# Sixteen transposes of the identity on TensorE ahead of the first real matmul of a graph network kernel

## What is computed

```
h = relu(layernorm(x));  x = x + attention(h, adj, W, a)      # scores e_i + e_j, leaky relu, masked softmax
h = relu(layernorm(x));  x = x + mlp((1 + eps) h + adj h)     # W1, b1, relu, W2, b2
h = relu(layernorm(x));  x = x + adj (h weight) + bias
h = relu(layernorm(x));  x = x + gru(h, adj)                  # five recurrent steps
```

## Time and profile before

| | us |
|---|---|
| median of three executions | 638.8 (637.78 to 640.11) |
| profiled execution, device time | 638.88 |
| its span, first to last instruction | 636.9 |
| TensorE busy | 607.4 (95%) |
| VectorE busy | 580.8 (91%) |
| ScalarE busy | 519.1 (82%) |
| GpSimd busy | 400.0 (63%) |

### The profile page before, as it was taken

The page is one execution under the profiler, slowest core; times in us unless marked ns, Lnnn a source line. Parts: engine busy times, 40 slices in busy tenths (PEclk is TensorE's granted clock), DMA queues, the critical chain, the costliest instruction groups (busy, mean ns, idle before and its releaser), DMA issues. The chain is left out here.

```text
span 636.9 us, 14522 instructions
## 1 busy us (share of the span) xinstructions
PE 607.4 (95%) x5070; PEld 386.6 (61%) x5070; DVE 580.8 (91%) x1390; ACT 519.1 (82%) x964; POOL 400.0 (63%) x361
## 2 busy tenths in 40 slices
PE   5899999999999999999999999999999999999994
PEld 3567778788888878555454455555455554555552
DVE  6678898989888888899989999999999999999996
ACT  3788899999999999687777787877877778787784
POOL 3456777778777877366577665555655556555564
PEclk9999999999999999999999999999999999999998
DMA  8101011110100000232322233343334334234342
GB/s 180 50 5 55 17 48 38 47 45 26 51 20 18 19 19 1 52 50 51 66 46 55 50 67 73 77 83 68 67 72 78 64 70 84 58 76 84 67 82 67
DMA packets 113642, 35.78 MB, mean 56 GB/s; under 512 B 86625, under 2 KB 113570, under 8 KB 113570
## 3 DMA queue, kind: packets, MB, share of 16 engines
q1 hardware_dynamic: 113424, 34.79, 25.6%
q10 hardware_dynamic: 146, 0.07, 0.0%
HBM read 9.67 MB, written 4.19 MB: 22 GB/s over the span
## 5 line engine op out<-in xcount | busy, mean ns | idle before, releaser
L1733 POOL TENSOR_TENSOR h0T<-r,zh 128x512 f32<-128x512 f32 x80 | 101.5, 1269 | 138.9 <-DVE r L1770 136.8
L52 PE MATMUL psum<-h_parts,gru_w 128*128 128x512 f16 x720 | 182.9, 379 | 4.4 <-DVE r L1774 4.4
L52 PE MATMUL psum<-t_parts,gru_w 128*128 128x512 f16 x720 | 181.5, 379 | 0.0
L52 PEld LDWEIGHTS psum<-h_parts,gru_w 128*128 128x128 f16 x720 | 69.3, 98 | 87.2 <-DVE r L1774 18.0
L1727 POOL TENSOR_TENSOR zh<-z,h0T 128x512 f32<-128x512 f32 x80 | 103.2, 1289 | 8.1 <-ACT z L1705 7.8
L52 PEld LDWEIGHTS psum<-t_parts,gru_w 128*128 128x128 f16 x720 | 66.7, 98 | 66.6 <-DVE t_parts L1757 7.4
L1702 ACT CAST t_parts<-psum 128x512 f16<-128x512 f32 x80 | 46.8, 585 | 61.1 <-PE psum L52 61.0
L1616 DVE CAST h_parts<-h0T 128x512 f16<-128x512 f32 x80 | 81.2, 1015 | 1.9 <-POOL h0T L1733 1.9
L1710 ACT ACTIVATE r<-r,gates_b 128x512 f32<-128x512 f32 x80 | 65.0, 812 | 14.2 <-DVE r L1761 11.1
L719 POOL TENSOR_TENSOR prob<-prob,row_max 128x512 f32<-128x512 f32 x64 | 64.5, 1040 | 10.9 <-DVE row_max L1326 10.4
L1705 ACT ACTIVATE z<-psum,gates_b 128x512 f32<-128x512 f32 x80 | 62.2, 778 | 5.8 <-PE psum L52 0.9
(11 more groups left out here) (147 smaller groups left out, 1115.3 us busy)
## 6 DMA issues: line engine op xcount, KB each, us to landing
x_all<-in_x SPq DMA_DIRECT2D x16, 256.0 KB, 4.7
adj<-in_adj SPq DMA_DIRECT2D x16, 256.0 KB, 3.0
out_x<-y SPq DMA_DIRECT2D x14, 256.0 KB, 2.5
h_nodes<-h_parts SPq DMA_TRANSPOSE x80, 3.1
out_x<-zT SPq DMA_DIRECT2D x2, 256.0 KB, 2.3
gw<-in_L_gnn_weight SPq DMA_DIRECT2D x1, 320.0 KB, 5.5
W<-in_L_gnn_W SPq DMA_DIRECT2D x2, 128.0 KB, 3.0
wi<-in_L_gnn_w_ih SPq DMA_DIRECT2D x1, 192.0 KB, 5.6
```

What stands on the lines that cost most here:

```text
L52: return nc.tensor.matmul(out, lhsT, rhs, start=start, stop=stop)
L1733: pool.tensor_tensor(state(now), by_graph(r[now.s][:, :]), by_graph(zh[now.s][:, :]), ALU.add)\
```

## The change

TensorE's slot 0 gets a function ahead of `spread_a`. It waits until `ident` is made and then transposes `ident` sixteen times into the first 128 columns of PSUM bank 2. Nothing reads the result, and no semaphore is raised by it.

```diff
+WARM_TURNS = 16
...
+        def warm_up():
+
+            pe.wait_ge(score_weights.eyes, 2)
+            for _ in range(WARM_TURNS):
+                nc.tensor.transpose(P[:, 2, 0:128], t["ident"][:, :], t["ident"][:, :])
+
...
         def slot(at, number):
             if number == 0:
+                warm_up()
                 score_weights.spread_a(pe)
             if number == 1:
                 score_weights.turn_max(pe)
```

## The result

Over ten executions each, the changed kernel takes 639.84 us (median; 638.97 to 640.83) and the one before 638.54 (637.43 to 640.11). The ratio is 1.0022 with a 95% interval of 1.0011 to 1.0032: slower by 1.3 us between the medians and 1.4 by the ratio, which is clear of noise and less than 0.3%. The forecast was +1.4 and 640.3. The profiled execution took 640.26 us, with a span of 638.3.

A forecast was written before the change was run, and what follows sets the result against it. TensorE was taken as the bound, busy for 95% of the span, with a start that is a chain from engine to engine. Delay +1.6 less 0.2 is +1.4 on 638.88, giving 640.3 us; range 637.8 to 642.0.

The forecast's parts named there:

- The delay: At L442, VectorE's take of `spread_a`'s result: start at 6.97 instead of 5.37, +1.6 us, +1.75 at most, +0.6 at least.
- the 2.05 us in hand: Between `spread_a`'s end at 3.32 and L442 at 5.37: the slack before a later `spread_a` delays VectorE.
- That it is passed on: Behind L442: VectorE, TensorE, ScalarE and GpSimd follow in turn, nothing takes the delay up, so it passes on in full.
- The two conditions together as less likely than not: TensorE's start: the burst must raise the clock and it must stay up; otherwise the delay remains, less a little.
- the first condition: At the burst of sixteen transposes: it must raise TensorE's clock.
- The second condition: Behind the burst: the clock must then stay up over a thin stretch of TensorE's work.
- the thin stretch that the prediction named: From `spread_a`'s end (6.9) to `turn_y0` (10.0): TensorE has only two small steps, the second of 0.58 us.
- The rule of the Trainium skill that I weighed: At the burst: transposes don't count as busy, so they wouldn't raise the clock; the sum is the delay alone, +1.6.
- If the rise comes at the same time as before: Clock rise at 17 to 18.3: work shifted by 1.6 meets it earlier; last transposes give back about 0.2.
- the exponential: ScalarE's, at 17.52 before: the prediction is wrong on the gain if it is not at about 19.
- The price of the levels: From 8 us on: a higher clock gains 1.2 us at the next slot; a later rise costs 1.4.
- the rival that ended slower: Clock rises later, after the transposes of prob and adj: delay 1.6 + 1.4 = +3.0, 641.9; chance 0.16.

The follow-up runs named there:

- the trace of 637.31: The kernel before, run again without an edit for a further trace; this execution took 637.31 us.
- the wait alone: Against the kernel before: no burst; `spread_a` waits instead for ScalarE's first logarithm. 640.09 us, ratio 1.0035 (1.0021 to 1.0049).
- the two traces with nearly the same clock: The kernel before in its execution of 637.31 us, and the kernel without a burst whose `spread_a` waits for ScalarE's first logarithm (640.09 us, ratio 1.0035).
- the trace of the changed kernel with spare transposes: The changed kernel plus thirteen spare transposes in TensorE's thin stretches: 639.46 us, ratio 1.0018 (1.0008 to 1.0029) against the kernel before.
- the burst behind and all thirteen spare ones: Changed kernel with the burst moved behind `spread_a`, plus six early and seven late spare transposes: 637.46 against 637.81 us of before, ratio 0.9986.
- the trace of before of 639.82: The kernel before, run again without an edit for a further trace; this execution took 639.82 us.
- The thirty-two: The changed kernel with thirty-two transposes instead of sixteen ahead of `spread_a`: 643.23 us, ratio 1.0081 (1.0067 to 1.0094) against the kernel before.
- the late spare ones without a burst: The kernel before plus seven spare transposes, behind the turn of gw and the first turn of prob: 637.96 us, ratio 0.9992 (0.9980 to 1.0004).

## Why the prediction was right, and where it was not

*The delay: right.* +1.6 at L442 was forecast, and 1.63 measured between the profiled executions. The pace and the start were right within 0.1 us (burst to 5.96, `spread_a` to 6.86). Over three traces each, L442 is at 6.64 and 5.07 in the mean, 1.57 apart. Single ones vary, since VectorE's statistics wait for the first x, and since a clock that rises within the burst shortens it; the 2.05 us in hand were 1.56 in the trace of 637.31. Moving the burst behind `spread_a` undoes the loss, and the wait alone reproduces it. That is shown.

*That it is passed on: right.* In the two traces with nearly the same clock, 2.03 us at L442 are 2.02 at `add_attended` and 2.1 in the span. Where the clock differs, its gain or loss comes on top.

*"The two conditions together as less likely than not": right as a whole, for a reason that I had only half.* The burst did raise the clock in all three traces of the changed kernel. But it is not sure to: with the same sixteen transposes at the same times, the trace of the changed kernel with spare transposes shows no rise, `spread_a` taking 1.22 and L427 0.37. So the first condition holds in three of four traces with the burst ahead of `spread_a`, and in all three with the burst behind it. The second condition failed each time: the clock fell again before 10 us in the three traces of the changed kernel, over the thin stretch that the prediction named. In the changed kernel nothing but sixteen transposes and the two one-row matmuls of `spread_a` came before the clock was up, L427 at 8.21 taking 0.27 instead of 0.37. The rule of the Trainium skill that I weighed (TensorE: Matmul & The Clock Gate, Part 4: PE-mode transpose), that transposes don't count as busy, does not hold for these f32 transposes; the measurement decides. The profile lists them as MATMUL, and no view says whether they run in the mode that the page means.

*"If the rise comes at the same time as before": wrong as a term.* I put -0.2 for it. There is no one time. In the first trace the clock was up by 13.4, and by the exponential, which I had put at 19, 1.46 had come back (lag of 1.63 down to 0.17). The fall at 20 took 1.35 away again (lag of 1.52 at `add_attended`). In sum 1.63 - 1.46 + 1.35 = 1.52. In the other two traces of the changed kernel the clock rose during the projection and did not fall at 20: from L442 to `add_attended` they take 19.94 and 19.93, where the first takes 20.81. So no run shows the -0.2, a rise at the time of before that meets the work 1.6 earlier. The net for the medians is about 1.57 - 1.3 = 0.3, and that this lies near the 0.2 is luck; the delay, the term that makes the sum, is not.

*The price of the levels: sizes about right.* The prediction had 1.2 us for a clock that is up from 8 us on. The trace with the burst behind and all thirteen spare ones has it up from the burst on, and takes 20.92 - 19.45 = 1.47 less from L442 to `add_attended` than the first trace of before. The trace of before of 637.31 has it up from about the projection on, and takes 1.18 less. It had 1.4 us for the transposes of prob and of adj at the lower level, in the rival that ended slower; the trace of before of 639.82 has `add_attended` 0.89 later than the first one though its L442 is 0.41 earlier, which gives 1.3. What was missed is that both already happen to the kernel before, as chance. Its executions lie near 637.5, 638.6 and 640.1.

*The thirty-two.* Its profiled execution is the lowest of the four, 642.79, and `add_attended` comes 3.82 later than in the first trace of before. Of these 2.89 are the delay at L442. The exponential is at 19.97, which is 11.71 behind L442, against 12.15 before, so 0.44 was given back ahead of it; behind it 10.14 against 8.77 went, so 1.37 was lost by the fall of the clock: 2.89 - 0.44 + 1.37 = 3.82. The median of the four is another 0.4 higher, and the median of before beside them (638.25) 0.6 lower than that first trace, which makes the 5.0. Why all four executions are so slow is open; no run separates that.

## What to carry to other kernels

Work put in front of an engine's first instruction is paid for as soon as it is longer than the time that this instruction has in hand; read that from when the engine that takes its result does so, over several executions (here 2.05, 1.56 and 1.64 us in three). In this kernel the warm-up work did no harm behind the first real instruction, and such work is worth only what the clock's level is worth at the place where the engine is on the chain; what is raised early and not kept up by work is gone by then, as it was here. And a single trace is one draw: compare clock and delay over several. Here the burst behind `spread_a`, with seven spare transposes later, is 0.15% faster than before (0.03 to 0.28%), and the burst as the change places it is 0.22% slower (0.11 to 0.32%). The faster one was not told from the late spare ones without a burst (ratio 0.9992, 0.9980 to 1.0004).

## What the runs showed of the hardware

Sixteen f32 transposes of the identity in a row raised TensorE's clock in six of seven traces with them: all three of the changed kernel and all three with the burst behind `spread_a`, where L427 took 0.27 us. In the seventh (the changed kernel with spare transposes) the burst was the same, 2.31 to 5.96, and L427 took 0.37. Thirty-two raised it in one trace; eight did not in one. In no trace without a burst was it up at L427 (0.37 in all five). The clock's changes fall at different times in executions of the same kernel (first rise by 12.5, between 15.5 and 17, and between 17 and 18.3 in three traces of before, by the durations), and between two of them, with L442 0.08 apart, the time differs by 2.5 us. PEclk prints 1.00 ahead of the first recorded change of level, though f32 transposes take 421 ns there, and 272 at the higher level. And a clock that has risen can fall with TensorE far from idle: in the changed kernel it was up from 18 to 20 us with 1.09 of 2 us busy and down from 20.2 on, and in the execution of before of 639.82 it was up from 17.6 to 19.0 with 0.77 of 1.4 us busy, and down by 20.6. Between those two, from 19.00 to 20.60, TensorE was busy for all 1.60 us with a mean PEclk of 0.72, so the fall came when it had been working without a gap again.
